# A four-layer kernel on one core: odd search units accumulate in place, half of the first feed-forward layer moves behind the search, and GpSimd writes two layer norms' outputs

## What is computed

```
x = x + attend(layernorm(x), softmax(q k^T of ctx))          # small
x = x + h(layernorm(x))**2 @ dq(w_proj).T                    # h = relu(. @ dq(w_fc).T), 1024 wide
x = x + expert(layernorm(x), fside, ctx)                     # two int8-like products with a silu between
x = x + product_keys(layernorm(x), Wq, keys, e_down, e_up)   # top 8 of 8 x 8 of 128 keys, 2048 experts
```

```
for s in linspace(0.4, 1.0, 16):
    scale = base * s
    deq = clip(round(w / scale), -15, 15) * scale
    err = sum((deq - w)**2)          # keep the scale with the least error
```

## Time and profile before

| | us |
|---|---|
| median of 3 runs | 424.01 |
| lowest, highest | 423.84, 425.61 |
| the profiled execution | 423.64 |
| its span, first to last instruction | 421.8 |
| PE busy in the span | 362.5 (86%) |
| DVE busy | 339.7 (81%) |
| ACT busy | 247.5 (59%) |
| POOL busy | 175.7 (42%) |

### The profile page before, as it was taken

The page is one execution under the profiler, slowest core; times in us unless marked ns, Lnnn a source line. Parts: engine busy times, 40 slices in busy tenths (PEclk is TensorE's granted clock), DMA queues, the critical chain, the costliest instruction groups (busy, mean ns, idle before and its releaser), DMA issues.

```text
span 421.8 us, 8486 instructions
## 1 busy us (share of the span) xinstructions
PE 362.5 (86%) x3278; PEld 272.1 (65%) x3278; DVE 339.7 (81%) x870; ACT 247.5 (59%) x371; POOL 175.7 (42%) x203
## 2 busy tenths in 40 slices
PE   2987897859979999799757797899878999999896
PEld 1553674525444554799646576788767888888785
DVE  4999689995997696646787899999978899999740
ACT  4889959967959898113655576757464766202000
POOL 3264635468988999500001004434124425404000
PEclk9998899989989999899986999999989999999899
DMA  8930000000000000330000000000000000000000
GB/s 253 363 119 2 0 0 2 0 1 2 0 0 2 0 0 1 101 101 2 1 0 2 1 0 2 3 2 2 12 4 4 11 14 5 12 3 14 2 14 26
DMA packets 11144, 11.42 MB, mean 27 GB/s; under 512 B 608, under 2 KB 10592, under 8 KB 11104
## 3 DMA queue, kind: packets, MB, share of 16 engines
q1 hardware_dynamic: 11104, 10.88, 8.1%
HBM read 9.83 MB, written 1.05 MB: 26 GB/s over the span
## 4 chain that ended last, share of the span: by engine, by line
PE 43%; DVE 34%; ACT 10%; issue 8%; POOL 4%; DMA 1%; POOLq 0%; DVEq 0%; ACTq 0%
PE pair L738 11%; PE pair L702 6%; PE pair L576 6%; PE pair L724 4%; POOL arena L336 3%; PE pair L537 3%; PE pair L515 2%; DVE arena L1567 2%; DVE i L1511 2%; PE pair L544 2%; DVE arena L1571 2%; DVE arena L1312 2%; DVE s L1505 2%; ACT arena L996 2%; PE pair L673 1%
## 5 line engine op out<-in xcount | busy, mean ns | idle before, releaser
L336 POOL TENSOR_TENSOR arena<-arena 128x512 f32<-128x512 f32 x64 | 90.9, 1430 | 50.7 <-ACT arena L996 19.9
L738 PE MATMUL pair<-EU,arena 128*128 128x256 f32 x256 | 60.9, 391 | 0.8 <-DVE arena L1595 0.6
L702 PE MATMUL pair<-arena,EDT 128*128 128x256 f32 x256 | 60.3, 386 | 0.0
L1312 DVE TENSOR_REDUCE arena<-arena 128x16 f32<-128x512 f32 x64 | 42.7, 678 | 19.1 <-POOL arena L336 19.0
L537 PE MATMUL pair<-QP,nidentr 128*128 128x512 f32 x144 | 46.5, 447 | 10.6 <-ACT arena L993 8.0
L738 PEld LDWEIGHTS pair<-EU,arena 128*128 128x128 f32 x256 | 48.6, 194 | 8.5 <-issue 1.7
L702 PEld LDWEIGHTS pair<-arena,EDT 128*128 128x128 f32 x256 | 47.9, 193 | 6.6 <-issue 0.2
L377 POOL TENSOR_TENSOR arena<-arena 128x512 f32<-128x512 f32 x20 | 30.4, 1531 | 48.5 <-ACT arena L1119 44.8
L537 PEld LDWEIGHTS pair<-QP,nidentr 128*128 128x128 f32 x144 | 27.0, 201 | 22.5 <-issue 14.9
L996 ACT ACTIVATE arena<-pair 128x1024 f32<-128x1024 f32 x32 | 33.4, 1043 | 12.2 <-PE pair L544 12.2
L544 PE MATMUL pair<-arena 128*128 128x512 fp8e4 x128 | 40.2, 397 | 0.0
(11 more groups left out here) (196 smaller groups left out, 655.5 us busy)
## 6 DMA issues: line engine op xcount, KB each, us to landing
...
```

The lines of the kernel that those rows point to most:

```text
L336: pool.tensor_tensor(qf(g), sq[:, :, 0:32], sq[:, :, 32:64], ALU.add).then_inc(s["folded"], 1)
L702: last = pe.matmul(bk2(4 + i % 2)[:, r, :], EDT[:, k, at:at + P], xT4[:, b % 2, k, :], start=(k == 0), stop=(k == 1))
L738: last = pe.matmul(bk2(7)[:, n, :], PR[:, n, e, :], EU[:, e, :], start=(e == 0), stop=(e == EROWS - 1))
L1312: dve.tensor_reduce(err[:, g // NS % 2, :, g % NS], qf(g), AX.X, ALU.add).then_inc(s["reduced"], 1)
```

## The change

1. `kept` holds for odd units too: only j = 0 and j = 1 of each chunk are written in full. `stepN` has 16 slots, and lies in the buffer of WQ1, whose load SP now issues after the last `sum_error`.
2. The outputs of the first two layer norms are made on GpSimd, two tiles of 128 x 256 per batch, ahead of the folds of units 4 to 7 and 21 to 24. DVE only takes the reciprocals.
3. The blocks of the first product are ordered by token half. The eight of batches 0 and 1 stand in the search at units 29, 33, ..., 57; the eight of batches 2 and 3 stand behind it, with buffers of their own (`hr_late`).
4. The maxima of the contexts (`m_w2`) move from unit 6 to behind the search.
5. The written-out lists behind the search are ordered anew on PE, ACT, DVE and POOL.

```diff
-        stepN = cut(6 * KI + 256, CH // 2, BF16).rearrange("p (j c) -> p j c", j=NS // 2)
+        stepN = WQ1[:, :, :].rearrange("p k c -> p (k c)").bitcast(BF16).rearrange("p (j c) -> p j c", j=NS)
...
-        FFN1_UNIT = {29 + 2 * i: i for i in range(2 * HID // P)}
+        FFN1_UNIT = {29 + 4 * i: i for i in range(HID // P)}
...
+        def hidden_block(i):
+
+            return i % (HID // P), i // (HID // P)
+
+        def hr(i):
+            return (hr_early if i < HID // P else hr_late)[:, i % 2, :]
...
+            sp.wait_ge(s["reduced"], NU)
             sp.dma_start(WQ1[:, :, :], wq1.rearrange("(n p) c -> p n c", p=P)).then_inc(ld["wq1"], 16)
-            sp.wait_ge(s["reduced"], NU)
...
+            def normalise(b, name):
+
+                for t in (2 * b, 2 * b + 1):
+                    ins = pool.tensor_scalar(XN[:, t, :], X[:, t, :], mv[:, t, 0:1], rstd[:, t:t + 1],
+                                             ALU.subtract, ALU.mult)
+                ins.then_inc(s[name], 1)
+
             for g in range(NU):
 
+                if 4 <= g < 4 + B:
+                    pool.wait_ge(s["ln1_inv"], 1)
+                    normalise(g - 4, "ln1")
+                if 21 <= g < 21 + B:
+                    pool.wait_ge(s["ln2_inv"], g - 20)
+                    pool.wait_ge(s["xT_t"], B)
+                    normalise(g - 21, "ln2")
...
+            square_hidden(8)
+            square_hidden(9)
...
-                m, half = i // 2, i % 2
-                pe.wait_ge(s["wT_e"], 2 if i < 8 else 4)
+                m, half = hidden_block(i)
+                pe.wait_ge(s["wT_e"], 2 if m < 4 else 4)
...
-                kept = j >= 2 and not on_act(g) and not on_act(g - 2)
+                kept = j >= 2 and on_act(g) == on_act(g - 2)
...
-                        pe.matmul(to[half], stepN[:, j // 2 - 1, :], qr[:, (g - 2) % QDEEP, cols[half]], start=False,
+                        pe.matmul(to[half], stepN[:, j - 2, :], qr[:, (g - 2) % QDEEP, cols[half]], start=False,
...
+            pe.wait_ge(s["wT_e"], 6)
+            ffn1(8)
+            ffn1(9)
+            ffn1(10)
             pe.wait_ge(s["squared"], NU)
-            pe.wait_ge(s["wT_e"], 6)
-            pe.wait_ge(s["hsq"], 16)
             gate_weights_transposed(0)
-            ffn2(1, 0)
+            pe.wait_ge(s["hsq"], 8)
             ffn2(0, 0)
...
-            for j in range(0, NS - 2, 2):
-                dve.tensor_scalar(stepN[:, j // 2, :], ident[:, :], -STEPS[j] / GRID, None, ALU.mult)
+            for j in range(NS - 2):
+                sign = 1.0 if on_act(j) else -1.0
+                dve.tensor_scalar(stepN[:, j, :], ident[:, :], sign * STEPS[j] / GRID, None, ALU.mult)
...
-                    ln_apply(0, NT, "ln1")
...
+                    dve.wait_ge(s["ln1_std"], 1)
+                    dve.reciprocal(rstd[:, :], rstd[:, :]).then_inc(s["ln1_inv"], 1)
...
-                    if g == 21 + b // 2:
-                        dve.wait_ge(s["xT_t"], B)
-                        ln_apply(b, 2, "ln2")
+                    if g == 20 + b // 2:
+                        dve.wait_ge(s["ln2_std"], b + 1)
+                        dve.wait_ge(s["ln1"], B)
+                        dve.reciprocal(rstd[:, 2 * b:2 * b + 2], rstd[:, 2 * b:2 * b + 2]).then_inc(s["ln2_inv"], 1)
```

439 lines of the change are left out of this document (235 added, 204 removed).

## The result

The changed kernel takes 420.88 us (median of four executions, 420.36 to 421.39) against 423.92 us for the kernel before on the same chip: a ratio of 0.992, 95% interval 0.989 to 0.995. It is faster by 0.8%, 3 us, where 12.5 us were forecast. Its profiled execution took 420.58 us, with a span of 418.8.

What follows compares the result with a forecast made beforehand. The prediction took PE to set the search's pace, with DVE's chunk hand-overs as second bound. From the profiled 423.64 us, -16 (search), +1 (its end) and +2.5 (PE behind it) gave 411.1 us, range 402 to 421.

Steps and rivals of the forecast that it cites:

- What bounds the kernel: Search: PE never pauses and sets the pace, 3.95 us per two units; DVE's chunk hand-overs are a second bound.
- Part 1: Odd units in the search: four matmuls (1.00 us) become two (0.43); stretch to the first hand-over zero, plus or minus 2.
- Part 2: Layer norms' products on GpSimd: 0.6 us a tile, 1.2 us per batch, hidden; DVE sheds 6.1 us.
- Hidden in POOL's idle 15.8 us: Second layer norm's products: 1.2 us per batch, four times, covered by POOL's idle 15.8 of 40.7 us.
- lost cover: Second layer norm's products, if not hidden: the last two transposes before the first layer wait about 2 us.
- Part 3: Search as a whole: stretches near their busiest engine's time, 94.7 us against 110.6, so -16, bounds -20 and -10.
- only half cured: Search, bad-side bound of -10: today's friction, over 6 us a chunk between DVE's busy time and the length, half remains.
- Part 4: End of the search: last choose and quantise run beside GpSimd's squares, 0 to 2 us, taken as +1.
- Part 5: PE behind the search: moved blocks mostly hidden in idle time, +2.5 us, bounds +12.3 and -3.
- The rest: Everything later: same PE and DVE instructions in a slightly different order, so zero.
- DVE takes PE's place and keeps its contention: Rival for the search: it gains only 10 us, total 417.1 us; chance 17%.
- the clock rival: Rival for the search: PE's clock falls to 1.2 GHz in plain pairs, kernel slower, 426 to 441 us; chance 7%.

Runs made afterwards that it cites:

- e9: e1 with all 16 first-layer blocks in the search and none behind it, cheaper odd units kept: 420.5 us, ratio 0.992.
- e10: The kernel before with only VectorE's prepare and scale of weight chunks 2 and 3 made earlier: 417.5 us, ratio 0.984.
- e3: The changed kernel with each first-layer block in the search cut in two steps, the second one unit later: 421.0 us, ratio 0.992.
- e1: The changed kernel with the products of both layer norms back on VectorE: 415.2 us, ratio 0.978.
- e6: e1 with eight buffers of folded errors instead of four and four of squares instead of three, from unit 24 on: 414.7 us, ratio 0.979.
- e13: The kernel before with only the new order behind the search, without the eight moved blocks: 421.0 us, ratio 0.993.
- e8: e13 plus the seven added constants, the later load of the query weights and the later maxima: 422.9 us, ratio 0.999.

## Why the prediction was wrong

**What bounds the kernel**: "PE never pauses, so it sets the pace". This was the first wrong step. An engine without a pause in a period can still be in step with others: GpSimd was at 37.1 of 39.7 us, and VectorE's hand-over added 4.1 us outside the period. e9 took work off TensorE and the chunk stayed at 39.5; e10 took none off it, moved VectorE's work, and the chunk fell to 36.4, GpSimd's busy time.

**Part 1** (odd units): the price per unit was right (0.59 pairs in place of 1.00), the forecast period of 6.6 us was not. It is 7.34, since the block stands between an odd and an even difference; with the block divided (e3) it is 6.35. The stretch up to the first hand-over is 2.5 us longer, outside the plus or minus 2. Part of that is the execution: e1 and e6, the same up to there, differ by 1.5 us (65.9 and 64.4).

**Part 2** (products): the term that was mis-sized. A tile is 1.22 us undisturbed and 1.58 in the mean where 0.6 was taken; it lies at the upper bound of 0.5 to 1.24, which came from rows of other forms. "Hidden in POOL's idle 15.8 us" failed too: idle time over a stretch says nothing about the few us in which TensorE waits for this tile. What is queued behind the waiting instruction was named for GpSimd and VectorE, not for TensorE, where it cost: 5.8 us instead of 0, against the 2 us named for lost cover.

**Part 3** (-16): the rule "a stretch cannot be shorter than its busiest engine" is true and was used as a forecast, with 0.8 to 2.4 us of friction. With the products on VectorE the friction was 7 us in each of the first two stretches (41.2 with ACT busy 34.3, 37.8 with VectorE 30.7; the earlier trace rows had 5.8 and, to GpSimd's 37.1, 2.6). The bound on the bad side, "only half cured", assumed a cure. GpSimd, at 37.1 of 39.7 us, is not in the sum. Without the products the change's parts give 9.2 us in all; the edit that cured the hand-over gave 5.7 us more.

**Part 4** (+1): 1.4 us, right. **Part 5** (+2.5): 4.2 us in the profile, of which the order by itself is 1.5 (57.9 us in e13 against 56.4). That the blocks are hidden was right. **The rest** ("zero") failed too, on the good side: 10.8 us less from the first top-8 on. The granted clock, 1.00 for 0.98, is the smaller part of it. At the same 0.98 as before, e1 with the new order takes 177.2 us there, 7.9 less, and e8, in its slowest execution, 179.9:

```profile
236.70:421.80 185.10, 167.32 (x2309) 142.37 (x2307) 154.98 (x499) 81.99 (x135) 51.64 (x68) 0.98 0.02 8
237.00:414.20 177.20, 165.59 (x2304) 141.32 (x2302) 154.40 (x499) 80.66 (x133) 51.79 (x68) 0.98 0.02 8
```

The second row is e1's. TensorE is idle 17.8 us in the first and 11.6 in the second. By the medians the order alone is worth 2.8 us (e13), less than this. In its profiled execution, which at 417.5 us is one of its fastest, the last part takes 176.0 us, 9.1 less, and some of that is lost ahead of the first top-8: the second stretch is 42.1 us for 40.7, in unchanged code at a clock of 0.88 for 0.96, and the one behind the last dequantise 1.5 longer.

**The rivals.** "DVE takes PE's place and keeps its contention" named the right neighbour at 417.1, and the clock rival was half right: the clock fell to 0.50 for 10 us in the search, in a stretch that runs low in several kernels with and without the change, and not in the plain pairs that it was argued from. The time within the range is luck. The upper end held by a hair because the products' 5.8 us and what else the search did not give were partly offset by the order, for which nothing was forecast.
